# Order of TensorE's steps in the opening: the first up-projection bank of tile 1 ahead of tile 0's rank, the second ahead of tile 1's router

## The chip, the cores and the metric

The kernel runs on one core of a Trainium2 chip. The metric is the time of one execution on the device in microseconds; shown are the median and the spread of several executions. The engines are named as in the profile: PE is TensorE's matmul, PEld its weight load, DVE is VectorE, ACT is ScalarE, POOL is GpSimd, SPq is the queue of SyncE, which issues most transfers.

## The reference

A block of one attention layer and one mixture-of-experts layer, both fed by the same normalised input, over 8 x 512 = 4096 tokens of width 256:

```python
xn = _layernorm(x)
x = x + attn(xn, k, v) + ffn(xn, ...)
# attn: softmax(einsum('bsd,btd->bst', xn, k) * scale) @ v, 1024 keys,
#       scale = xn[:, ::s//4] laid out over the keys
# ffn:  shared = gelu(xf @ Wfc_s + bfc_s) @ Wproj_s + bproj_s       (256 -> 1024 -> 256)
#       probs = softmax(xf @ Wr);  top 2 of 8 experts, weights renormalised
#       routed = sum over e of (gelu(xf @ Wfc[e] + bfc[e]) @ Wproj[e] + bproj[e]) * gate[:, e]
#       return shared + routed
```

## The kernel before

The tokens are cut into 16 tiles of 256. Every float32 product is done as three float16 products: each operand is split into a high and a low half (high x high, high x low, low x high), which the code calls TERMS. The work has stages: for tiles 0 to 7 the shared expert with the routing; attention for 32 blocks of 128 tokens, in whose gaps the other tiles are routed and the expert weights are split and packed; the routed experts over 43 steps of gathered tokens; then the shared expert for tiles 8 to 15. Each engine has its own program written out by hand, and they meet only at semaphores; there is no planner. TensorE's program order is what the change edits.

For each tile of the first stage these steps follow one another over the engines:

- VectorE takes the statistics (front_a with stat), GpSimd the power, VectorE normalises (normalize), ScalarE and VectorE write the high and low half of the rows (split_x_hi, split_x_lo).
- TensorE transposes the tile into PSUM (tr1), and it is copied to x_t: by ScalarE for tiles 0 and 1 (in tile 1's case the copy at L892), by VectorE for the others.
- TensorE does the router's small matmuls (router, L1476). VectorE finds the top two experts and makes a mask (front_a with route, the mask at L1030).
- TensorE does the rank (rank, L1487 to L1490): five matmuls of 8 columns which count, for each token, how many tokens before it go to the same expert. It waits for the mask. VectorE turns this into slot numbers (slots_first at L1053 and L1054, then slots_rest to L1069), and GpSimd scatters the rows (L753).
- TensorE does the up-projection (up_shared, L1513) in four banks of PSUM, each of two hidden chunks and 12 matmuls of 256 columns. ScalarE takes the GELU of each bank and its high half (L858, L864), VectorE the low half (split_h, L1086).
- TensorE does the down-projection. For tile 0 it is cut up in down_first (L1592): the first two terms of each half tile need the high halves of the weights, the third needs their low half, which VectorE makes in split_w1_lo (L1113, two pieces of w_shared[1]; the second one is released to TensorE by s_wlo).

The ps_h bank of a tile may be written again when the GELU of the same bank of the tile before has read it (s_gelu). keep_busy(n) issues n matmuls of 128 columns on the identity, whose result nobody reads.

VectorE's program for the stretch in question, in its order, is:

```python
split_h(0, 0, banks=(0,)); split_x_lo(1)
front_a(route=0); split_w1_lo(0); front_b(route=0)      # front_b: slots_first(0), slots_rest(0)
split_h(0, 0, banks=(1,)); front_a(stat=2); split_h(0, 0, banks=(2, 3))
front_a(route=1); normalize(2); split_h(1, 1, banks=(0,)); split_x_lo(2)
split_w1_lo(1); slots_first(1); copy_xt(2)
```

ScalarE's, from the same point: split_x_hi(1), both scalings of the down weights (L889, L890), the copy of tile 1's x_t (L892), then the GELUs of tile 0's banks 1, 2 and 3, then tile 1's banks 0 and 1, split_x_hi(2) and banks 2 and 3.

Of the kernel before, what the change touches and what calls it, by code (L numbers as in the profile page):

```python
# [68 lines left out]
def moe_attention_block(nc, q, k, v, wfc_s, bfc_s, wproj_s, bproj_s, wr, wfc, bfc, wproj, bproj, out):  # L69
# [30 lines left out]
    with ctx:  # L100
# [1343 lines left out]
        def _(pe):  # L1444
# [14 lines left out]
            def tr1(i):  # L1459
                pe.wait_ge(s_hl, 2 * i)  # L1460
                if i:
                    pe.wait_ge(s_xt, i)
                transpose_quads(x_split[i % 3]).then_inc(s_tr, 1)
# [6 lines left out]
            def router(i, bank=misc):  # L1470
                pe.wait_ge(s_xt, i + 1)
                if 0 < i < NA:
                    pe.wait_ge(s_rb, RB * (i - 1) + 2)
                for a in range(SUB):
                    for n in range(2 * DC):
                        ins = mm(lg_ps(bank)[:, a * 16:(a + 1) * 16], x_t[:, i, n, a * P:(a + 1) * P], wr_s[:, n % DC, :],  # L1476
                                 start=n == 0, stop=n == 2 * DC - 1)
                ins.then_inc(s_logit, 1)

            def rank(i, bank=misc):  # L1480
                par = i % 2
                pe.wait_ge(s_ra, (i + 1) * RA)
                if i:
                    pe.wait_ge(s_rb, (i - 1) * RB + 3)
                for a in range(SUB):
                    o = rk_ps(bank)[:, a * EXPERTS:(a + 1) * EXPERTS]
                    mm(o, before[:, :], mask[par][:, a, :], start=True, stop=False)  # L1487
                    if a == 1:
                        mm(o, ones_h[:, :], mask[par][:, 0, :], start=False, stop=False)
                    ins = mm(o, ones_h[:, :], mask_sum[:, :], start=False, stop=True)  # L1490
                ins.then_inc(s_rank, 1)
# [10 lines left out]
            def up_banks(t, x, w, banks, cols=TILE):  # L1502
                wv = w[:, :].rearrange("p (h c n) -> p h c n", h=2, c=DC)
                for b in banks:
                    if isinstance(t, int) and t == R0:
                        pe.wait_ge(s_mul, QT - 1 + b // 2)
                    elif not (isinstance(t, int) and t == 0):
                        pe.wait_ge(s_gelu, BANKS * (t - 1) + b + 1)
                    for hc in (2 * b, 2 * b + 1):
                        n = 0  # L1510
                        for wl, xl in TERMS:
                            for c in range(DC):
                                ins = mm(ps_h[:, hc * TILE:hc * TILE + cols], wv[:, wl, c, hc * P:(hc + 1) * P],  # L1513
                                         x[:, xl * DC + c, 0:cols], start=n == 0, stop=n == 3 * DC - 1)
                                n += 1
                    ins.then_inc(s_mm1, 1)

            def up_shared(i, t, banks=range(BANKS)):
                pe.wait_ge(s_xt, i + 1)
                up_banks(t, x_t[:, i, :, :], w_shared[0], banks)  # L1520
# [28 lines left out]
            def keep_busy(count):  # L1549

                for n in range(count):
                    mm(ps_v[:, 0:P], ident_h[:, :], ident_h[:, :], start=True, stop=True)
# [23 lines left out]
            router(0)  # L1576
            up_shared(0, 0, (3,))
            tr1(1)
            keep_busy(9)
            rank(0)  # L1580
            keep_busy(6)
            up_shared(1, 1, (0,))
            router(1)

            def down_first(a, terms):
# [7 lines left out]
                                 start=n == 0 and c == 0, stop=n == 2 and c == HC - 1)  # L1593
                return ins

            up_shared(1, 1, (1, 2, 3))
            pe.wait_ge(s_whi, 1)
            down_first(0, (0, 1))
            rank(1)
# [203 lines left out]
```

## Time and profile before

| what | value |
| --- | --- |
| median of 3 runs | 752.18 us (751.36 to 752.41) |
| the profiled execution | 751.78 us |
| its span in the trace | 750.0 us |
| TensorE busy | 738.9 us, 99% of the span |
| VectorE busy | 460.0 us, 61% |
| ScalarE busy | 452.2 us, 60% |
| GpSimd busy | 232.1 us, 31% |

The profiled execution's own time is 1.78 us more than its span. The shares of busy time are averages over all stages; the change lies within the first 30 us. In the rows below, a timeline row has the start and the length in us, the engine, the line, the operation, the tiles written and read, the shapes, and xN for N instructions merged; in brackets is how long the engine had been idle before and what it was released by. The ends of matmuls are modelled, so a row of matmuls overlaps the next one by the time that the last of them takes to drain: the time that a group holds the engine is from its start to the start of the next.

### The profile page before, as it was taken

The page shows a single profiled execution, that of the slowest core. Times are in us where ns is not written, and L with a number is a line of the kernel's source. Part 1 is how long each engine was busy: PE and PEld are TensorE (multiplying, and loading weights), DVE is VectorE, ACT ScalarE, POOL GpSimd, SP SyncE. Part 2 cuts the span into 40 slices and gives each one's busy share as a digit, 9 for nine tenths or more (in the row PEclk, how much of TensorE's full clock was granted, in tenths as well). Part 3 has the DMA queues.
Part 4 walks back from the last instruction along what each step waited for, and adds up shares of the span by engine and source line. Part 5 has one row for each costly group of instructions (what it writes and reads, how often), then busy time and mean ns, then how long its engine had stood idle before and what let it go on. Part 6 is the DMA issues. An engine that isn't in the chain of part 4 may idle for free.

```text
span 750.0 us, 21773 instructions
## 1 busy us (share of the span) xinstructions
PE 738.9 (99%) x7280; PEld 632.5 (84%) x7280; DVE 460.0 (61%) x1200; ACT 452.2 (60%) x903; POOL 232.1 (31%) x275
## 2 busy tenths in 40 slices
PE   6999999999999999999999999999999999999998
PEld 6899977777777777999999999899888888888887
DVE  6888868877777786445454455455444445437766
ACT  6766547666668775466564666665555445554452
POOL 3545426666665663012121211222121221220000
PEclk9999999999999999999999999999999999999999
DMA  9656132748575979554522667533646466205464
GB/s 307 222 187 172 38 141 88 263 160 278 172 248 176 315 257 305 158 170 119 162 49 56 192 190 210 140 103 85 198 136 199 119 177 206 90 27 171 147 211 155
DMA packets 101360, 127.43 MB, mean 170 GB/s; under 512 B 58832, under 2 KB 82992, under 8 KB 94896
## 3 DMA queue, kind: packets, MB, share of 16 engines
q1 hardware_dynamic: 77104, 105.08, 45.7%
q0 software_dynamic: 6368, 17.31, 6.4%
q10 hardware_dynamic: 17824, 4.23, 2.9%
q8 instruction: 35, 0.57, 0.3%
q14 instruction: 29, 0.24, 0.1%
HBM read 85.73 MB, written 40.85 MB: 169 GB/s over the span
## 4 chain that ended last, share of the span: by engine, by line
PE 95%; DVE 2%; ACT 1%; issue 1%; DMA 0%; POOL 0%; DVEq 0%; ACTq 0%; POOLq 0%
PE ps_h L1513 33%; PE ps_v L1533 33%; PE ps_v L1692 11%; PE ps_h L1630 11%; PE ps_t L1644 4%; PE ps_v L1711 1%; PE ps_v L1455 0%; PE ps_t L1455 0%; DMA acc<-in_L_attn_q_dram 0%; ACT h L858 0%; DVE xn L1038 0%; POOL rstd L729 0%; DVE w_shared L1113 0%; PE ps_v L1592 0%; DVE h_split L1086 0%
## 5 line engine op out<-in xcount | busy, mean ns | idle before, releaser
L1086 DVE TENSOR_TENSOR h_split<-h,h_split 128x512 f16<-128x512 f32 (+2 forms) x236 | 140.5, 602 | 138.2 <-ACT h_split L864 136.8
L858 ACT ACTIVATE h<-ps_h,b_fc 128x256 f32<-128x256 f32 (+2 forms) x344 | 127.9, 422 | 141.6 <-PE ps_h L1513 141.5
L1513 PE MATMUL ps_h<-x_t,w_split 128*128 128x256 f16 (+2 forms) x2064 | 185.2, 250 | 1.4 <-DVE x_t L1315 1.2
L1513 PEld LDWEIGHTS ps_h<-x_t,w_split 128*128 128x128 f16 x2064 | 163.8, 98 | 17.5 <-DVE x_t L1315 1.1
L1533 PE MATMUL ps_v<-w_stage,h_split 128*128 128x256 f16 x1536 | 173.6, 273 | 0.0
L799 POOL DMA_INDIRECT tokens_y<-prob,to_i x71 | 73.0, 1028 | 314.1 <-DVE prob L1352 148.9
L1533 PEld LDWEIGHTS ps_v<-w_stage,h_split 128*128 128x128 f16 x1536 | 149.9, 98 | 17.1
L864 ACT CAST h_split<-h 128x512 f16<-128x512 f32 (+2 forms) x236 | 130.1, 551 | 10.6
L1692 PE MATMUL ps_v<-v_split,p_t 128*128 128x256 f16 x768 | 88.9, 272 | 0.0
L1630 PE MATMUL ps_h<-k_t,x_t 128*128 128x512 f16 x384 | 88.1, 379 | 0.0
L858 ACT ACTIVATE h<-ps_h,b_t 128x256 f32<-128x256 f32 x128 | 53.5, 468 | 55.5 <-PE ps_h L1513 55.3
L1513 PE MATMUL ps_h<-x_t,w_shared 128*128 128x256 f16 x756 | 85.4, 273 | 0.0
L1533 PE MATMUL ps_v<-w_shared,h_split 128*128 128x256 f16 x720 | 82.0, 273 | 0.0
L1692 PEld LDWEIGHTS ps_v<-v_split,p_t 128*128 128x128 f16 x768 | 73.6, 98 | 9.8
L1513 PEld LDWEIGHTS ps_h<-x_t,w_shared 128*128 128x128 f16 x756 | 73.3, 98 | 8.4
L1533 PEld LDWEIGHTS ps_v<-w_shared,h_split 128*128 128x128 f16 x720 | 70.2, 98 | 8.5
L753 POOL DMA_INDIRECT slots_x<-x_split,pos_i x64 | 64.7, 1011 | 26.7 <-issue 12.7
L1630 PEld LDWEIGHTS ps_h<-k_t,x_t 128*128 128x128 f16 x384 | 37.6, 98 | 38.1
L912 ACT ACTIVATE prob<-prob,neg_max 128x1024 f32<-128x1024 f32 x32 | 36.8, 1149 | 51.6 <-DVE neg_max L1194 51.6
L1190 DVE CUSTOM_DVE_ANT_0 prob<-ps_h,scale_b 128x1024 f32<-128x1024 f32 x32 | 39.1, 1223 | 23.1 <-PE ps_h L1630 22.9
L1352 DVE SCALAR_TENSOR_TENSOR prob<-ps_v,b_pj 128x256 f32<-128x256 f32 x64 | 26.6, 422 | 36.6 <-PE ps_v L1533 36.1
L1315 DVE STREAM_TRANSPOSE x_t<-x_split 128x1024 f16<-128x1024 f16 (+2 forms) x43 | 43.4, 1009 | 0.0
(184 smaller groups left out, 635.1 us busy)
## 6 DMA issues: line engine op xcount, KB each, us to landing
w_split<-wpack SPq DMA_DIRECT2D x17, 1024.0 KB, 5.6
w_stage<-wpack SPq DMA_DIRECT2D x17, 1024.0 KB, 5.4
wpack<-w_split SPq DMA_DIRECT2D x8, 1024.0 KB, 5.0
wpack<-h_split SPq DMA_DIRECT2D x8, 1024.0 KB, 5.3
y_rows<-tokens_y SPq DMA_DIRECT2D x32, 256.0 KB, 3.2
w_stage<-in_L_ffn_Wfc_dram SPq DMA_DIRECT2D x4, 1024.0 KB, 7.2
scale_b<-key_scale SPq DMA_DIRECT2D x8, 512.0 KB, 8.0
w_stage<-in_L_ffn_Wproj_dram SPq DMA_DIRECT2D x4, 1024.0 KB, 8.4
```

The source lines that it names most:

```text
L753: g.indirect_dma_start(slots_x, bass.IndirectOffsetOnAxis(ap=pos_i[par][:, c:c + 1], axis=0), x_split[i % 3][:, a, :], None).then_inc(s_sc ...
L799: g.indirect_dma_start(tokens_y, bass.IndirectOffsetOnAxis(ap=to_i[par][0:p, a:a + 1], axis=0), y_sb[par][0:p, a, :], None).then_inc(s_y_o ...
L858: ins = nc.scalar.activation(h32[:, hc, 0:n], ps_h[:, hc * TILE:hc * TILE + n], ACT.Gelu_apprx_tanh, bias=bias[:, hc:hc + 1], scale=1.0 / WS)
L864: nc.scalar.copy(h_split[par][:, 0, 2 * b:2 * b + 2, 0:n], h32[:, 2 * b:2 * b + 2, 0:n]).then_inc(s_hhi, 1)
L912: nc.scalar.activation(prob[par][:, :], prob[par][:, :], ACT.Exp, bias=neg_max[par][:, 0:1], accum_out=row_sum[par][:, 0:1]).then_inc(s_ex ...
L1086: ve.tensor_tensor(h_split[par][:, 1, 2 * b:2 * b + 2, 0:n], h32[:, 2 * b:2 * b + 2, 0:n], h_split[par][:, 0, 2 * b:2 * b + 2, 0:n], ALU.s ...
L1190: ve.tensor_tensor_reduce(out=prob[par][:, :], in0=ps_h[:, par * KEYS:(par + 1) * KEYS], in1=scale_b[b % 2][:, :], scale=1.0, scalar=-3.0e ...
L1315: ve.transpose(x_t[:, par, :, 0:n].rearrange("p c (b t) -> p b c t", t=32), x_quad[par][:, 0:n // 32, :].rearrange("p b (r c) -> p b c r", ...
L1513: ins = mm(ps_h[:, hc * TILE:hc * TILE + cols], wv[:, wl, c, hc * P:(hc + 1) * P], x[:, xl * DC + c, 0:cols], start=n == 0, stop=n == 3 * ...
L1533: ins = mm(ps_y[a][:, :], h_split[par][:, xl, c, a * P:(a + 1) * P], wv[:, wl, c, :], start=n == 0, stop=n == 3 * HC - 1)
L1630: ins = mm(ps_h[:, lo:lo + 512], x_t[:, i, ql * DC + c, par * P:(par + 1) * P], k_t[:, kl * DC + c, half * 512:(half + 1) * 512], start=n ...
L1692: ins = mm(ps_y[par][:, :], p_t[par][:, pl, c, :], v_split[:, vl, c, :], start=n == 0, stop=n == 3 * KC - 1)
```

## The change

In TensorE's program for tiles 0 and 1, nine fillers ahead of rank(0) become eighteen, the six behind it go, bank 0 of tile 1 moves from behind rank(0) to ahead of it, and bank 1 of tile 1 from behind router(1) to ahead of it. No instruction of another engine changes.

```diff
             tr1(1)
-            keep_busy(9)
+            keep_busy(18)
+            up_shared(1, 1, (0,))
             rank(0)
-            keep_busy(6)
-            up_shared(1, 1, (0,))
+            up_shared(1, 1, (1,))
             router(1)
...
-            up_shared(1, 1, (1, 2, 3))
+            up_shared(1, 1, (2, 3))
             pe.wait_ge(s_whi, 1)
             down_first(0, (0, 1))
```

## Rows read from the trace of the kernel before

**Rows 1.** The page: its span, and the chain's shares by engine.

```profile
span 750.0 us, 21773 instructions
...
PE 95%; DVE 2%; ACT 1%; issue 1%; DMA 0%; POOL 0%; DVEq 0%; ACTq 0%; POOLq 0%
```

**Rows 2.** What TensorE waited for, whole span: us in total, times, longest.

```profile
PE ps_h L1513 <- DVE x_t L1315: 1.2, 2, 1.0
...
PE ps_t L1487 <- DVE mask L1030: 0.7, 1, 0.7
PE ps_v L1592 <- DVE w_shared L1113: 0.5, 1, 0.5
PE ps_t L1455 <- DVE x_split L1044: 0.3, 1, 0.3
```

**Rows 3.** Timeline of PE, 9 to 29 us.

```profile
9.62 1.48 PE L1565 MATMUL ps_h<-x_t,w_shared 128*128 128x256 f16 x12 [0.99 <-ACT x_t L878]
...
15.71 0.67 PE L1552 MATMUL ps_v<-ident_h 128*128 128x128 f16 x9
17.08 0.18 PE L1487 MATMUL ps_t<-mask,before 128*128 128x8 f16 x1 [0.70 <-DVE mask L1030]
...
17.19 0.17 PE L1490 MATMUL ps_t<-mask_sum,ones_h 128*128 128x8 f16 x1
...
17.55 1.47 PE L1513 MATMUL ps_h<-x_t,w_shared 128*128 128x256 f16 x12
18.86 0.35 PE L1476 MATMUL ps_t<-wr_s,x_t 128*128 128x16 f16 x8
...
22.99 1.91 PE L1592 MATMUL ps_v<-w_shared,h_split 128*128 128x256 f16 x16
...
27.04 0.64 PE L1455 MATMUL ps_t<-ident_h,x_split 128*128 128x128 f16 x8 [0.27 <-DVE x_split L1044]
28.18 1.92 PE L1592 MATMUL ps_v<-w_shared,h_split 128*128 128x256 f16 x16 [0.49 <-DVE w_shared L1113]
```

**Rows 4.** Timeline of all engines, 16 to 28 us: those of DVE and ACT.

```profile
16.19 0.99 ACT L892 COPY x_t<-ps_t 128x1024 f16<-128x1024 f16 x1
...
17.08 0.84 ACT L858 ACTIVATE h<-ps_h,b_t 128x256 f32<-128x256 f32 x2
...
17.95 0.62 ACT L864 CAST h_split<-h 128x512 f16<-128x512 f32 x1
18.07 0.16 DVE L1053 TENSOR_TENSOR mask_sum<-mask_sum,mask 128x8 f16<-128x8 f16 x1
...
19.15 0.69 DVE L1086 TENSOR_TENSOR h_split<-h,h_split 128x512 f16<-128x512 f32 x1
...
21.05 0.18 DVE L1015 BATCH_NORM_AGGREGATE mean_var<-stats 128x2 f32<-128x6 f32 x1 [0.27 <-issue]
...
21.42 1.29 DVE L1086 TENSOR_TENSOR h_split<-h,h_split 128x512 f16<-128x512 f32 x2
...
24.49 0.18 DVE L1030 TENSOR_TENSOR mask<-chosen 128x16 f16<-128x16 f32 x1
...
26.29 0.70 DVE L1044 TENSOR_TENSOR x_split<-xn,x_split 128x512 f16<-128x512 f32 x1 [0.28 <-ACT x_split L840]
26.90 1.22 DVE L1113 SCALAR_TENSOR_TENSOR w_shared<-w_stage,w_shared 128x1024 f16<-128x1024 f32 x1
```

**Rows 5.** The chain that ended last, 16 to 29 us: start, us, what.

```profile
17.02 1.14 DVE w_shared L1113
...
26.99 1.14 DVE w_shared L1113
```

**Rows 6.** Fillers by form, 15.6 to 19.2 and 4 to 8 us: busy us, mean ns.

```profile
L1552 PE MATMUL ps_v<-ident_h 128*128 128x128 f16 x15 | 1.2, 219 | 0.0
...
L1540 PE MATMUL ps_v<-ident_h 128*128 128x128 f16 x31 | 3.5, 313 | 4.2 <-POOL ends L723 4.2
```

**Rows 7.** Windows, 26 to 30 us: busy by engine, granted clock, DMA share, GB/s.

```profile
26.00:30.00 4.00, 3.24 (x35) 2.57 (x33) 3.72 (x9) 2.90 (x7) 2.65 (x2) 1.00 0.44 119
```

## The prediction

> **What bounds the kernel now.** I read the page first, for its span and the chain of work that ended last: TensorE carries 95% of the chain [rows 1]. Then the list of what TensorE waited for. Everything on it but the first wait for constants, at 4.17 us, lies either in the opening or at one point of the routed stage: 1.0 us before tile 0's first up-projection [rows 3], 0.7 us for tile 0's mask, 0.3 us for tile 2's split rows, 0.5 us for the low half of the shared down weights, and 1.2 us for gathered slots far later [rows 2]. Asked for waits from 30 to 400 us, the trace lists none for TensorE. So from 28.18 us on, where the third terms of tile 0's down-projection start, TensorE is dense, and what moves that start moves the end of the kernel by the same amount. The one later wait hangs on engines and transfers that are themselves paced by TensorE's steps, so it moves along and swallows nothing.
>
> Then the opening in order of time. TensorE ends its fillers, waits 0.70 us for the mask, does the five small matmuls of rank(0) at 17.08, six more fillers, bank 0 of tile 1 at 17.55, router(1) at 18.86, the rest of tile 1's banks, and reaches down_first at 22.99; at 27.04 and at 28.18 it stands waiting for VectorE [rows 3]. VectorE in the same stretch goes from one thing to the next [rows 4]. The chain, followed back from 28.18, runs on VectorE: the low half of w_shared[1] at 26.99 is its last piece before TensorE, and from the other half at 17.02 the trace follows it through slots_first(0), the splits of h, the statistics and normalisation of tile 2, with one step over ScalarE (its high half of tile 2's rows) and none over TensorE [rows 5]. So in the opening between 17 and 28 us VectorE sets the pace and TensorE has 0.27 + 0.49 = 0.76 us to spare.
>
> **The change part by part.** (1) Bank 0 of tile 1 moves ahead of rank(0). It needs tile 1's x_t, which ScalarE's copy from 16.19 gives at 16.19 + 0.99 = 17.18 [rows 4]. A step of TensorE that waits for another engine's result starts 0.05 to 0.06 us behind its end (28.12 to 28.18, 26.99 to 27.04 [rows 3, 4]), so bank 0 starts at 17.24 in place of 17.55. Its other condition, the GELU of tile 0's bank 0, is met: ScalarE takes bank 1 at 17.08, and bank 0 stands far ahead of the copy in its program. Gain for TensorE: 0.31 us.
>
> (2) keep_busy(18) in place of 9 and 6. Nine fillers span 0.67 us, of which the last one's own time is 0.22 [rows 3, 6]: 0.45 over eight starts, 0.056 each. Eighteen started at 15.71 take 17 x 0.056 + 0.22 = 1.17 us and end at 16.88, 0.36 us ahead of the copy. They cost nothing; what hides them is that wait. If the fillers went at the slow rate of the first 31 (3.5 us less 0.31, over 30 starts: 0.106 each [rows 6]), the last would start at 17.5 and bank 0 at about 17.6, which would make term 3 worse by 0.37. I don't expect it, since the same fillers in the same place ran at the fast rate. The six fillers behind rank(0) go, 6 x 0.056 = 0.33 us of TensorE time.
>
> (3) rank(0) now stands behind bank 0. A bank's twelve matmuls hold TensorE for 18.86 - 17.55 = 1.31 us [rows 3], so rank(0) starts at 17.24 + 1.31 = 18.55 in place of 17.08, and its last record ends 17.19 + 0.17 - 17.08 = 0.28 us later, at 18.83, in place of 17.36. Who waits for it: slots_first(0) on VectorE, that stands directly behind split_w1_lo(0) in its queue. Before, it started at 18.07 [rows 4], 0.71 us after rank(0) had ended, so the result had that much to spare. Now it can start at 18.83 + 0.05 = 18.88. VectorE stands idle and is 18.88 - 18.07 = **0.81 us late**. Queued behind it are slots_rest(0), the split of h of bank 1 (19.15), tile 2's statistics, the splits of banks 2 and 3, tile 1's routing, and the rest of the chain above.
>
> Is there slack in that queue? The split of bank 1 has its input from ScalarE at 17.95 + 0.62 = 18.57 and yet starts at 19.15, behind the slots [rows 4]; VectorE passes nothing. The Trainium skill, "TensorE: Matmul & The Clock Gate", section "Architectural detail: the array is 16× 32×32, not 1× 128×128", says that VectorE's queue is strictly first in, first out; by that rule the whole 0.81 us is lost, whereas a queue that could pass the waiting step would fill it with the 0.68 us split and lose only 0.13. The trace agrees with the rule at that place. The splits of banks 2 and 3 start at 21.42 with no idle before them; normalize(2) needs GpSimd's power, which is made out of VectorE's own variance, and the 0.28 us before 26.29 is the round trip over ScalarE; both move along. The single gap that need not move is 0.27 us at 21.05, put down to the issue and to no other engine [rows 4]. If it is tied to the clock on the wall (something fetched ahead that the new idle time lets arrive), it is swallowed and the delay is 0.81 - 0.27 = 0.54 us. If it belongs to the instruction it stays. I take it as staying, because the row names no releaser; both ends are kept for the range.
>
> (4) Bank 1 ahead of router(1). Bank 1 starts at 18.55 + 0.14 = 18.69 (its GELU of tile 0's bank 1 must have been read, a step that lasts from 17.08 to 17.92) and router(1) at 20.00 in place of 18.86. Its logits are read by VectorE behind the splits that start at 21.42 and last 1.29, so at about 22.7 before and 23.5 now: covered by more than 3 us, and nothing is late if that cover shrinks by one. Banks 2 and 3 run until 20.00 + 0.2 (router(1)'s 0.35 less the drain of its last) + 2 x 1.31 = 22.82 in place of 22.99.
>
> (5) What TensorE then does. down_first(0) needs all splits of tile 0's h: 21.42 + 1.29 + 0.81 = 23.52, so it starts at 23.57 in place of 22.99 and lasts until 25.3. rank(1) needs the mask that ended at 24.67 [rows 4], now 25.48. The transposes of tile 2 need the split that ended at 26.99, now 27.80, so they start at 27.85; and the third terms need split_w1_lo(1), which ended at 28.12 and now ends at 28.93: start at 28.99 in place of 28.18. TensorE has four short stands in this stretch in place of two, none above 0.7 us, and the 0.31 us and 0.33 us it gained go into them. **Sum:** gain on TensorE 0, VectorE's delay +0.81, end of the kernel +0.81 us, or +0.54 with the gap swallowed.
>
> No transfer is on this way: GpSimd's row ends and scatters of tile 0 start 0.8 us later, but nothing reads the slots before the routed stage. The queue of SyncE has its next loads released by VectorE (the next job's weights behind split_w1_lo(1)) and moves along.
>
> **How the numbers follow.** The profiled execution took 751.78, that is 1.78 us around its span of 750.0. Span 750.0 + 0.81 + 1.78 = 752.59. The median of the runs shown, 752.18, lies 0.40 above the profiled one, and on it the same sum gives 752.99. I predict 753.0. The three runs shown spread over 1.05 us, so from what a measurement can tell, some 0.2% or 1.5 us, this is no change, though on the slow side.
>
> **Rival A, TensorE paces the opening.** If VectorE's lateness were hidden (its queue having slack that the rows don't show, or rank(0) not on its way), the start at 28.18 would follow TensorE's own order, and it would be 0.17 to 0.31 us earlier: 751.9 to 752.0. For it speaks only that TensorE is busy in 95% of the chain; against it that the chain in the opening has no piece of TensorE between 17 and 28 us, and that TensorE stands idle twice in front of VectorE. Chance 0.14, mixtures of the two included.
>
> **Rival B, on the other side: the clock falls.** TensorE now idles more between 22.8 and 29.0: 0.76 us before and about 1.7 us now. If that made its clock fall to the lower of its two levels (1.2 GHz), the dense work behind 29 us would start slow. At the lower level a 128-column filler takes 313 ns and 0.106 us from start to start, at the upper (2.4 GHz) 219 ns and 0.056 us [rows 6]. The slow fillers of the opening last 3.5 us; work for as long as this at the slow rate would lose 3.5 x (1 - 0.056/0.106) = 1.65 us. With the 0.81 this is +2.5, 754.7, slower by 0.3%. It decides when one of the new stands, or their sum, is enough for the clock to fall. Against it: the granted clock is 1.00 from 26 to 30 us in spite of the two stands there [rows 7], and the 0.99 us stand before the first up-projection was followed by twelve matmuls in 1.48 us, as fast as the 1.47 of bank 0 at 17.55 [rows 3]; my longest new stand is 0.7. The Trainium skill, same page, section "HAM oscillation — how this bites in real kernels", warns that stands between short bursts put the clock back to half rate; it speaks of longer ones than I forecast, and by it the change costs nothing here. Chance 0.07.
>
> Other ways to a slower end, a second fetch gap or a transfer that the shift of 0.8 us brings into collision, I give 0.05; and the forecast itself, VectorE late by 0.54 to 0.81 us, has 0.74.
>
> **Chances and range.** Forecast case: 752.7 to 753.0, with a median's own scatter of about 0.5 on either side 752.2 to 753.6. Rival A reaches down to 751.4 with that scatter; rival B lies at 754.7. The range of 8 in 10, 751.6 to 754.2, holds the forecast, most of A, and leaves out B. Over 0.2% faster (under 750.7) no case gives, only scatter: 0.03. Over 0.2% slower (above 753.7): B, the other slower ways and the forecast's upper scatter: 0.07 + 0.02 + 0.04 = 0.13. Within 0.2%: 0.84.
>
> **What would show it.** In the profile of the changed kernel: bank 0 of tile 1 at about 17.24 with a short wait for ScalarE's x_t ahead of it; rank(0) at 18.55 with no wait; a new wait of VectorE's mask_sum for TensorE's rank of about 0.75 us; the wait for the mask gone from TensorE's list and one for h_split of about 0.7 in front of down_first at 23.6; the third terms at 29.0. If the mask_sum step starts at 18.9 but the third terms start before 28.6, VectorE had slack that I didn't see; if they start before 28.2, rival A holds. A 256-column mean well over 272 ns behind 29 us would be rival B. The prediction is wrong altogether if the time past 29 us changes by more than the opening does.

## The result, and the profile after

| | before | after |
| --- | --- | --- |
| median of 20 runs each | 751.77 us (751.3 to 752.73) | 752.59 us (752.06 to 756.64) |
| span of the profiled execution | 750.0 us | 750.9 us |
| TensorE busy | 738.9 us | 739.2 us |

The ratio is 1.0013 with a 95% interval of 1.0007 to 1.0019; the medians differ by 0.82 us. That is slower, but inside the 0.2% that the prediction called no change, and on its slow side. Ratios and intervals, here and below, leave out single slow executions (1999.31 us for one) and are taken over all the others, so they need not be the quotient of two medians. The page of the changed kernel gives the span:

```profile
span 750.9 us, 21780 instructions
```

The list of TensorE's waits over the whole span, without its first row (the constants). The 0.7 us for the mask [rows 2] is gone. In its place stand 0.7 us for the splits of h in front of down_first and 0.4 us for tile 1's x_t; the 0.5 us for the low half of the weights is still there. Far later, in the routed stage, 0.2 us for a transfer of weights is new, while the waits for gathered slots fell from 1.2 to 1.0:

```profile
...
PE ps_h L1513 <- DVE x_t L1315: 1.0, 1, 1.0
PE ps_h L1565 <- ACT x_t L878: 0.9, 1, 0.9
PE ps_v L1592 <- DVE h_split L1086: 0.7, 1, 0.7
PE ps_t L1455 <- DVE x_split L1044: 0.6, 2, 0.3
PE ps_v L1592 <- DVE w_shared L1113: 0.5, 1, 0.5
PE ps_h L1513 <- ACT x_t L892: 0.4, 1, 0.4
PE ps_h L1513 <- DMA w_split<-wpack: 0.2, 1, 0.2
```

The timeline of PE, against [rows 3]:

```profile
15.80 1.17 PE L1552 MATMUL ps_v<-ident_h 128*128 128x128 f16 x18
17.32 1.48 PE L1513 MATMUL ps_h<-x_t,w_shared 128*128 128x256 f16 x12 [0.35 <-ACT x_t L892]
18.64 0.17 PE L1487 MATMUL ps_t<-mask,before 128*128 128x8 f16 x1
...
18.75 0.17 PE L1490 MATMUL ps_t<-mask_sum,ones_h 128*128 128x8 f16 x1
...
20.08 0.35 PE L1476 MATMUL ps_t<-wr_s,x_t 128*128 128x16 f16 x8
20.28 2.78 PE L1513 MATMUL ps_h<-x_t,w_shared 128*128 128x256 f16 x24
23.73 1.91 PE L1592 MATMUL ps_v<-w_shared,h_split 128*128 128x256 f16 x16 [0.67 <-DVE h_split L1086]
...
27.93 0.64 PE L1455 MATMUL ps_t<-ident_h,x_split 128*128 128x128 f16 x8 [0.27 <-DVE x_split L1044]
29.06 1.92 PE L1592 MATMUL ps_v<-w_shared,h_split 128*128 128x256 f16 x16 [0.50 <-DVE w_shared L1113]
30.82 0.35 PE L1476 MATMUL ps_t<-wr_s,x_t 128*128 128x16 f16 x8
```

The timeline of all engines, those of VectorE, against [rows 4]:

```profile
17.02 1.22 DVE L1113 SCALAR_TENSOR_TENSOR w_shared<-w_stage,w_shared 128x1024 f16<-128x1024 f32 x1
...
18.95 0.16 DVE L1053 TENSOR_TENSOR mask_sum<-mask_sum,mask 128x8 f16<-128x8 f16 x1 [0.71 <-PE ps_t L1490]
...
20.04 0.69 DVE L1086 TENSOR_TENSOR h_split<-h,h_split 128x512 f16<-128x512 f32 x1
...
21.93 0.18 DVE L1015 BATCH_NORM_AGGREGATE mean_var<-stats 128x2 f32<-128x6 f32 x1 [0.27 <-issue]
...
22.30 1.28 DVE L1086 TENSOR_TENSOR h_split<-h,h_split 128x512 f16<-128x512 f32 x2
...
27.17 0.70 DVE L1044 TENSOR_TENSOR x_split<-xn,x_split 128x512 f16<-128x512 f32 x1 [0.28 <-ACT x_split L840]
27.78 1.22 DVE L1113 SCALAR_TENSOR_TENSOR w_shared<-w_stage,w_shared 128x1024 f16<-128x1024 f32 x1
```

And two rows of the kernel before, of VectorE's first w_shared piece and of router(2):

```profile
16.94 1.22 DVE L1113 SCALAR_TENSOR_TENSOR w_shared<-w_stage,w_shared 128x1024 f16<-128x1024 f32 x1
```

```profile
29.93 0.35 PE L1476 MATMUL ps_t<-wr_s,x_t 128*128 128x16 f16 x8
```

How to read them: this execution is 0.08 us later than the one before from the start of the stretch (w_shared at 17.02 against 16.94), so each shift below is measured from that row. mask_sum comes 0.80 us later, with a new wait of 0.71 for the last matmul of the rank; the split of bank 1 0.81 later; the second piece of the low half and TensorE's third terms 0.80 later. I call D the distance from VectorE's first w_shared piece to the third terms: 28.18 - 16.94 = 11.24 us before, 29.06 - 17.02 = 12.04 now. And R is the distance from the same row to router(2), from which on TensorE is dense up to the routed stage: 30.82 - 17.02 = 13.80 now, 29.93 - 16.94 = 12.99 before.

One view of the changed kernel misleads. Its chain of work that ended last no longer runs on VectorE throughout; it steps over to ScalarE:

```profile
17.27 0.75 ACT h L858 x2
...
18.66 0.75 ACT h L858 x2
...
20.05 0.67 DVE h_split L1086
```

The split at 20.04 is that of bank 1. The cast that it needs is ScalarE's of bank 1, which ended before 18.7. The trace follows it back to the next cast, bank 2's, only because that one ended at 20.05. By the chain alone one would look for the loss on ScalarE. The experiments below tell where it is.

### The profile page after: what moved, and what is told of

Read it like the earlier page. It is cut to its first block, busy times and chain, and to the rows that moved or that the text cites. A ratio compares the mean times of both kernels' runs of the same rounds, so it can differ in the third digit from the quotient of the medians.

```text
span 750.9 us, 21780 instructions
## 1 busy us (share of the span) xinstructions
PE 739.2 (98%) x7283; PEld 632.1 (84%) x7283; DVE 460.0 (61%) x1200; ACT 451.7 (60%) x903; POOL 233.5 (31%) x275
## 4 chain that ended last, share of the span: by engine, by line
PE 93%; DVE 2%; ACT 2%; DMA 1%; issue 1%; SPq 1%; POOL 0%; DVEq 0%; POOLq 0%; ACTq 0%
PE ps_h L1513 32%; PE ps_v L1533 32%; PE ps_v L1692 11%; PE ps_h L1630 11%; PE ps_t L1644 4%; DMA w_split<-wpack 1%; PE ps_v L1711 1%; ACT h L858 1%; PE ps_v L1455 0%; DMA acc<-in_L_attn_q_dram 0%; PE ps_t L1455 0%; POOL rstd L729 0%; DVE xn L1038 0%; ACT h_split L864 0%; PE ps_v L1592 0%
```

## The experiments

Each was timed beside the kernel before on the same chip, whose median was 751.98 us (30 runs) for the first four, 751.89 (35) for the next four and 751.82 (33) for the last four; the three groups ran on three different chips. D and R come from one profiled execution of each kernel. Line numbers of a changed file can be off by one or two (L1591, L1593 for L1592).

| kernel | median, us (lowest) | ratio, 95% interval | D | R |
| --- | --- | --- | --- | --- |
| bank1_only | 752.16 (751.60) | 1.0002, 0.9993 to 1.0011 | 11.39 | 13.14 |
| bank0_only | 752.55 (752.10) | 1.001, 1.0 to 1.0019 | 12.04 | 13.79 |
| rank_behind_two | 753.69 (753.43) | 1.0029, 1.0019 to 1.004 | 13.35 | |
| stat_first | 751.40 (751.11) | 0.9996, 0.9986 to 1.0005 | 11.14 | 12.90 |
| no_fill | 752.37 (752.07) | 1.001, 0.9999 to 1.0021 | 12.04 | 13.80 |
| tail_before | 750.72 (750.57) | 0.9988, 0.998 to 0.9997 | | 11.94 |
| tail_stat | 750.49 (750.31) | 0.9986, 0.9977 to 0.9995 | | 11.76 |
| fill_gap | 751.35 (751.25) | 0.9994, 0.9985 to 1.0002 | 11.23 | 12.99 |
| change_gap | 752.16 (752.02) | 1.0005, 0.9996 to 1.0015 | 12.03 | 13.78 |
| stat_first_gap | 751.04 (750.81) | 0.9988, 0.9978 to 0.9997 | 10.93 | 12.69 |
| tail_before_gap | 750.57 (750.42) | 0.9983, 0.9974 to 0.9993 | | 11.95 |
| tail_stat_gap | 750.37 (750.24) | 0.9985, 0.9975 to 0.9994 | | 11.77 |

**One part at a time.**

```diff
# bank1_only, against the kernel before
-            up_shared(1, 1, (0,))
+            up_shared(1, 1, (0, 1))
             router(1)
...
-            up_shared(1, 1, (1, 2, 3))
+            up_shared(1, 1, (2, 3))
# bank0_only, against the changed kernel
             rank(0)
-            up_shared(1, 1, (1,))
             router(1)
...
-            up_shared(1, 1, (2, 3))
+            up_shared(1, 1, (1, 2, 3))
```

> One part alone: rank(0) and its fillers stand as before the change, only bank 1 of tile 1 goes ahead of router(1). I measure in the trace the distance D from the start of VectorE's first w_shared[1] low half (17 us) to the start of TensorE's third terms of tile 0's down-projection: 11.24 us before the change, 12.04 after it. Theory (VectorE's wait for rank(0) is the whole loss): no wait of mask_sum for the rank, D 11.2, time within 0.3 us of the kernel before, ratio 1.000. Rival (it is the later router(1), whose logits VectorE reads, that costs): router(1) starts at about 20.2 in place of 18.86 here as well, and D is 12.0, time +0.8 us.

> The other part alone: eighteen fillers, bank 0 of tile 1, rank(0), then router(1) and banks 1, 2, 3. Theory: mask_sum waits 0.7 us for the rank as after the change, D 12.04, time +0.8 us, ratio 1.001. router(1) must now wait for slots_first(0), so TensorE stands about 0.45 us there, but it still reaches down_first before the splits of h are ready, so that costs nothing. Rival (TensorE's own order paces the opening): that stand adds to the loss, D 12.4 to 12.5, time +1.2 us. Rival (the later router(1) is the cost): D 11.3.

bank1_only costs nothing that can be measured (its interval is 0.1% to either side): VectorE's mask_sum (18.80, right behind w_shared at 17.66) has no wait, although router(1) came at 21.29, later than in the changed kernel. D is 11.39, 0.15 above that of the kernel before. That execution had a late start of another kind (last section): ScalarE copied x_t only at 17.59, its cast of bank 1 ended at 19.99, and VectorE's split of that bank, which follows the start of pos_i by 0.08 before, followed it by 0.22. bank0_only has the whole loss. Timelines of its VectorE and TensorE:

```profile
18.86 0.16 DVE L1053 TENSOR_TENSOR mask_sum<-mask_sum,mask 128x8 f16<-128x8 f16 x1 [0.71 <-PE ps_t L1490]
```

```profile
19.25 0.34 PE L1476 MATMUL ps_t<-wr_s,x_t 128*128 128x16 f16 x8 [0.43 <-DVE slot_of L1054]
...
28.97 1.92 PE L1591 MATMUL ps_v<-w_shared,h_split 128*128 128x256 f16 x16 [0.49 <-DVE w_shared L1113]
```

TensorE loses another 0.43 us in front of router(1), and D is 12.04 all the same: an idle TensorE costs nothing here. It also shows what bank 1 ahead of router(1) does in the change: it fills this stand, without a gain.

**The cost enlarged and taken away.**

```diff
# rank_behind_two, against the changed kernel
-            up_shared(1, 1, (0,))
+            up_shared(1, 1, (0, 1))
             rank(0)
-            up_shared(1, 1, (1,))
             router(1)
# stat_first, against the changed kernel, VectorE's program
             split_w1_lo(0)
+            front_a(stat=2)
             front_b(route=0)
             split_h(0, 0, banks=(1,))
-            front_a(stat=2)
```

> The suspected cost is enlarged: banks 0 and 1 of tile 1 both stand ahead of rank(0). Theory: rank(0) comes one more bank, 1.31 us, later, the wait of mask_sum grows from 0.71 to about 2.0 us, D 12.04 + 1.31 = 13.35, time 1.31 us above the changed kernel and +2.1 us above the one before, ratio 1.0028. Rival (the lateness is partly swallowed, the gap of 0.27 us in VectorE's issue first): D 13.1 or less. Rival (TensorE paces the opening, which does the same work in the same time): D stays near 12.0.

> TensorE's order as in the changed kernel, but VectorE does the statistics of tile 2 (about 1.67 us of its time with their pauses, needing nothing of the rank) ahead of slots_first(0) in place of behind the split of bank 1. Theory: they run from 18.1 to 19.8, the rank is ready at 18.9, mask_sum waits for nothing, and D is back at 11.2 to 11.3, time as the kernel before, ratio 1.000. Rival (the loss lies in TensorE's order itself, its clock or a transfer that comes later): D stays at 12.0 and the time at +0.8 us.

rank_behind_two, its timelines of VectorE and TensorE:

```profile
17.14 1.22 DVE L1113 SCALAR_TENSOR_TENSOR w_shared<-w_stage,w_shared 128x1024 f16<-128x1024 f32 x1
...
20.38 0.16 DVE L1053 TENSOR_TENSOR mask_sum<-mask_sum,mask 128x8 f16<-128x8 f16 x1 [2.02 <-PE ps_t L1490]
...
23.36 0.18 DVE L1015 BATCH_NORM_AGGREGATE mean_var<-stats 128x2 f32<-128x6 f32 x1 [0.27 <-issue]
```

```profile
25.16 1.91 PE L1591 MATMUL ps_v<-w_shared,h_split 128*128 128x256 f16 x16 [1.38 <-DVE h_split L1086]
...
30.49 1.70 PE L1591 MATMUL ps_v<-w_shared,h_split 128*128 128x256 f16 x14 [0.49 <-DVE w_shared L1113]
```

The wait grows by 2.02 - 0.71 = 1.31 us, which is one bank, and D by 13.35 - 12.04 = 1.31. Nothing of it is swallowed, and the gap of 0.27 us in front of the second aggregation is still there. The median is 1.71 above the kernel before where 2.1 was expected; the medians carry a scatter of half a microsecond, and lowest against lowest (753.43 against 751.34) it is 2.09.

stat_first keeps TensorE's order and gives VectorE other work during the wait. Its timelines of VectorE and of TensorE:

```profile
17.41 1.22 DVE L1113 SCALAR_TENSOR_TENSOR w_shared<-w_stage,w_shared 128x1024 f16<-128x1024 f32 x1
18.55 0.42 DVE L997 BATCH_NORM_STATS2 stats<-acc 128x6 f32<-128x256 f32 x1
...
19.75 0.17 DVE L1022 TENSOR_SCALAR var_eps<-mean_var 128x2 f32<-128x2 f32 x1
20.03 0.16 DVE L1053 TENSOR_TENSOR mask_sum<-mask_sum,mask 128x8 f16<-128x8 f16 x1
...
21.28 0.17 DVE L1069 CAST pos_i<-pos_all 128x4 int32<-128x4 f32 x1 [0.34 <-DVE pos_all L1067]
```

```profile
19.83 0.17 PE L1490 MATMUL ps_t<-mask_sum,ones_h 128*128 128x8 f16 x1
```

D is 11.14, below the 11.24 of the kernel before. No wait for the rank is listed, but this execution started late (last section): its rank ended only at 19.83 + 0.17 = 20.00, mask_sum follows at 20.03, and it stands 0.28 us behind the start of var_eps. In stat_first_gap (below), the same order without the late start, the rank has ended at 18.81, mask_sum follows var_eps by 0.08, and D is 10.93:

```profile
19.25 0.17 DVE L1022 TENSOR_SCALAR var_eps<-mean_var 128x2 f32<-128x2 f32 x1
19.33 0.16 DVE L1053 TENSOR_TENSOR mask_sum<-mask_sum,mask 128x8 f16<-128x8 f16 x1
```

So 0.2 us of the wait for the rank is left in stat_first, and none in its twin. The loss is gone with this wait though TensorE's order is the changed one: neither ScalarE nor TensorE's order as such holds it.

**The fillers.**

```diff
# no_fill, against the changed kernel
-            keep_busy(18)
```

> The changed kernel without its eighteen fillers, so TensorE stands idle for about 1.1 us ahead of bank 0 of tile 1. Theory (the fillers lie wholly in the wait for x_t and cost nothing): bank 0, rank(0) and the third terms where the changed kernel has them, D (first w_shared[1] low half to the third terms) 12.0 us, time within 0.4 us of the changed kernel, ratio to the kernel before 1.001; the clock stays, 256-column matmuls at 272 ns. Rival (the fillers are what keeps the clock at its upper level there): matmuls of 419 ns behind the stand, which the first up-projection has in some executions, in bank 0 and behind it, and D 13 or more.

Its timeline of TensorE, and its matmuls by form from 17 to 24 us:

```profile
17.12 1.48 PE L1513 MATMUL ps_h<-x_t,w_shared 128*128 128x256 f16 x12 [1.36 <-ACT x_t L892]
```

```profile
L1513 PE MATMUL ps_h<-x_t,w_shared 128*128 128x256 f16 x48 | 5.7, 272 | 1.4 <-ACT x_t L892 1.4
```

With 1.36 us of idle time ahead of bank 0 the clock stayed at its upper level (2.4 GHz), 272 ns for a 256-column matmul. In this execution the eighteen fillers bring nothing, and they cost nothing: the lowest times are 752.07 without and 752.06 with them. It is one profiled execution; that the clock stays in every one isn't shown.

**What VectorE's queue is worth at the other end.**

```diff
# tail_before, against the kernel before; tail_stat has the same edit on stat_first
# VectorE
             normalize(2)
+            split_w1_lo(1)
+            split_x_lo(2)
             split_h(1, 1, banks=(0,))
-            split_x_lo(2)
-            split_w1_lo(1)
# TensorE
-            tr1(2)
             pe.wait_ge(s_wlo, 2)
-            for a in range(SUB):
-                down_first(a, (2,)).then_inc(s_mm2, 1)
+            down_first(0, (2,)).then_inc(s_mm2, 1)
+            tr1(2)
+            down_first(1, (2,)).then_inc(s_mm2, 1)
```

> The kernel before, with only the end of the stretch changed: VectorE does split_w1_lo(1) directly behind normalize(2), in place of the split of h and its wait for ScalarE, and the split of tile 1's bank 0 behind split_x_lo(2); TensorE puts the transposes of tile 2 between the two halves of the third terms. I measure R, from the start of VectorE's first w_shared[1] low half to router(2) on TensorE: 12.99 us before, 13.80 in the changed kernel. Theory (VectorE's queue ahead of the third terms is what TensorE waits for, and from router(2) on TensorE is dense to the end): third terms without a wait, router(2) about 1.0 us earlier, R 12.0, time -1.0 us, 751.0, ratio 0.9987. Rival (the time is given back behind router(2)): R 12.0 but time within 0.3 us of the kernel before.

> The changed kernel's order on TensorE, with tile 2's statistics ahead of slots_first(0) and the end of the stretch as in tail_before. Theory: no wait for the rank on VectorE, and TensorE's earlier bank 0 at last counts, as long as the splits of h are ready at 22.8: R 11.8 to 12.0, time -1.0 to -1.3 us against the kernel before, some 1.9 us below the changed kernel. Rival (the earlier bank 0 is worth nothing whatever VectorE does): R as in tail_before, 12.0.

The timeline of TensorE in tail_before, where the third terms of the first half follow without a wait (24 matmuls in one row), and that of tail_stat:

```profile
24.86 2.78 PE L1592 MATMUL ps_v<-w_shared,h_split 128*128 128x256 f16 x24
27.48 0.61 PE L1455 MATMUL ps_t<-ident_h,x_split 128*128 128x128 f16 x8
27.93 1.04 PE L1592 MATMUL ps_v<-w_shared,h_split 128*128 128x256 f16 x8
28.88 0.36 PE L1476 MATMUL ps_t<-wr_s,x_t 128*128 128x16 f16 x8
...
37.26 0.64 PE L1455 MATMUL ps_t<-ident_h,x_split 128*128 128x128 f16 x8
...
40.36 0.35 PE L1476 MATMUL ps_t<-wr_s,x_t 128*128 128x16 f16 x8
```

```profile
28.75 0.36 PE L1476 MATMUL ps_t<-wr_s,x_t 128*128 128x16 f16 x8
```

router(2) comes 12.99 - 11.94 = 1.05 us earlier. Not all of it is kept: by router(3) 0.84 us is left (40.36 against the row below of the kernel before, each from its w_shared at 16.94). The transposes of tile 3, at 37.26, now start right behind VectorE's split of that tile, which ends at 36.51 + 0.70 = 37.21; before the change this split had ended 0.86 us before they started.

```profile
41.20 0.35 PE L1476 MATMUL ps_t<-wr_s,x_t 128*128 128x16 f16 x8
```

From there to the end of attention nothing more is lost. The medians give 1.17 us, with their scatter; the twins fill_gap and tail_before_gap below, which scatter less, give 751.35 - 750.57 = 0.78. So what is won in VectorE's queue reaches the end but for the 0.2 us for which VectorE is in the way again one tile later. tail_stat adds another 0.18 at router(2).

**The scatter.** In two of the first six profiled executions (the kernel before, the changed one and the first four experiments) the first up-projection had been slow, and this looked like the source of the 1.2 us over which the times of one kernel spread.

```diff
# fill_gap, against the kernel before; the other _gap kernels have the same line
+            keep_busy(9)
             up_first()
```

> The kernel before with nine more fillers ahead of tile 0's first up-projection, in its stand of 0.99 us. In two of six profiled executions the first twelve 256-column matmuls took 419 ns each, in the others 273, and tile 1's transposes then came 1.5 us later and the third terms 0.4 to 0.9 later. Theory (in those executions the clock has not yet risen when the up-projection starts, and more work ahead of it helps it to rise): 273 ns, the lowest time stays near 751.4 and the upper half of the runs (752.0 to 752.6) comes down, median 751.5 or 0.4 us below the kernel before. Rival (when the clock rises does not depend on this stand): the same scatter, same median.

The eleven runs lie between 751.25 and 751.45; those of the kernel before in the same session, one at 755.33 aside, between 751.32 and 752.59. With so little scatter, the change can be priced by times alone:

> The changed kernel with the nine fillers of fill_gap ahead of the first up-projection. Since these took the scatter out of the kernel before (751.25 to 751.45 in 11 runs), the cost of the change can be read from the times themselves: theory 751.35 + 0.81 = 752.16, all runs within 752.0 to 752.4, D (first w_shared[1] low half to the third terms) 12.04 us. Rival (part of the 0.8 is scatter or is given back later): 751.7 or less, or a spread as wide as without the fillers.

> The changed kernel with the nine fillers and tile 2's statistics ahead of slots_first(0). Theory: the wait for the rank is gone, D back at 11.0 to 11.2 us (the 0.27 us issue gap at the second aggregation was not in the trace of stat_first), so 751.35 or up to 0.2 us below it: 751.15 to 751.35. Rival (the change costs something beside the wait for the rank): above 751.6.

change_gap is 752.16 - 751.35 = 0.81 us above fill_gap, the predicted size. That it agrees to the hundredth is luck: the two ran on different chips, and measured from the kernel before on its own chip each, they are 0.34 + 0.54 = 0.88 apart. Nine of change_gap's eleven runs lie between 752.02 and 752.43, the others at 752.80 and, far outside, 2754.95. stat_first_gap is 751.04, 1.12 below change_gap on the same chip, where D differs by 1.10; and its D of 10.93 is 0.30 below that of fill_gap. So its reordering does more than take the wait of 0.8 us away: it also makes VectorE's queue 0.30 us shorter than before the change, which was not expected in this size. The two traces have 0.14 us of it up to tile 1's logits (5.54 us behind w_shared in place of 5.68), 0.12 from there to the mask (1.75 in place of 1.87) and 0.05 from there to the next split of h. The same instructions follow one another faster; why is open.

> The order before the change, the nine fillers, and the end of the stretch as in tail_before. Theory: 751.35 less the 1.04 us that tail_before gained at router(2): 750.3 to 750.6, with the scatter gone. Compared with tail_stat_gap it prices the change's earlier bank 0 once nothing on VectorE is in its way.

> The changed kernel's order with the nine fillers, tile 2's statistics first and the end of the stretch as in tail_before. Theory: TensorE is dense from bank 0 of tile 1 on, which starts at 17.2 with the x_t copy; router(2) comes at 28.6 to 28.75 (28.88 in tail_before, 28.75 in tail_stat), so 0.1 to 0.3 us below tail_before_gap: 750.1 to 750.4, the fastest of all. Rival (the earlier bank 0 is worth nothing whatever VectorE does): equal to tail_before_gap within 0.05.

750.57 and 750.37, 0.20 us apart, with R 11.95 and 11.77, 0.18 apart. So the change's earlier bank 0 has a value, 0.2 us, once VectorE is out of the way: TensorE is dense from bank 0 to router(2) in both, and bank 0 starts 0.31 behind w_shared in place of 0.61, from which rank(0) behind it takes about 0.13 again. And tail_stat_gap is the fastest kernel by its median: 1.8 us below the changed kernel's twin change_gap, and 0.15% (interval 0.06 to 0.25%) below the kernel before. By the intervals it can't be told from tail_before_gap.

## Why the prediction was right, point by point

- The bound: right. TensorE dense from the third terms on, VectorE's queue setting their start. The 0.80 us of D appear as 0.82 in the medians and 0.81 to 0.88 between change_gap and fill_gap. For a gain it holds only in part: of the 1.05 us of tail_before 0.84 is left one tile later.
- Parts 1 and 2: bank 0 at 17.32 - 0.08 = 17.24, as predicted; eighteen fillers in 1.17 us, as worked out. That they cost nothing holds; in no_fill's profiled execution they kept nothing either.
- Part 3, the term that decides: 0.81 predicted, 0.80 in the trace, with a wait of 0.71 where 0.75 stood. VectorE followed the rank's last record by 0.03 us, not 0.05. The choice between 0.81 and 0.54 was right: the gap at the second aggregation stayed at 0.27 us behind the new idle time. rank_behind_two confirms it at 2.02 us of idle.
- Part 4: router(1) at 20.00 on the scale of before, as predicted. bank1_only shows that its cover holds.
- Part 5: third terms at 28.98 on that scale, 28.99 predicted. down_first was put at 23.57, 0.05 behind the last split of h, and came at 23.65, 0.15 behind the split's end (22.30 + 1.28 to 23.73); it isn't shown why, and it costs nothing, since TensorE stands twice more behind it. Of the stands, "none above 0.7" doesn't fit the prediction's own figures, by which the one before down_first is 23.57 - 22.82 = 0.75; it was 0.67.
- That the waits of the routed stage swallow nothing was argued, not worked out. The two executions agree with it: 720.1 us from router(2) to the end in both, with 1.2 us of waits there in both, though 0.2 us of them is now for a transfer where the prediction saw none on the way. Over all kernels this distance is less constant (last section).
- Rival A, TensorE paces the opening: excluded. bank0_only adds 0.43 us of idle TensorE at no cost. Its price for the earlier bank 0 (0.17 to 0.31) is near what the two tail kernels give, 0.2, but only with VectorE's queue shortened.
- Rival B, the clock: did not happen. The stands in the changed kernel are 0.67, 0.27 and 0.50 us in the second half of the stretch, and matmuls of 256 columns take 272 to 273 ns behind them, as in no_fill behind 1.36 us.
- The absolute time, 753.0 against 752.59, was 0.4 too high. The term that was off is the base: the median of the three runs shown, 752.18, lay in the upper part of the scatter, and over 20 runs it is 751.77. 751.77 + 0.81 is 752.58. The profiled execution's sum hits 752.59 exactly, which is luck: that execution, at 751.78, happened to lie at the median of the 20.

## What to carry to other kernels

When a step of one engine is moved behind another, look up when its result is taken, not how long the step lasts: five matmuls of 8 columns, 0.28 us, cost 0.8 us, because a full queue stood behind the wait for them, while the 0.31 us that TensorE gained went into later waits. The chain of waits points at one releaser and can be wrong by a coincidence of ends; moving work that needs nothing ahead of the suspected wait (stat_first) tests it without touching the producer, but look at the whole queue again, since a new order can change more than the wait (0.30 us here). And where the effect is of the size of the scatter, measure distances between two rows of one trace, and look for what makes the scatter.

## What the runs showed of the hardware that was not expected

**A part of the scatter comes from when the clock rises.** The matmuls of the first up-projection by form, 8.5 to 11.9 us, in bank1_only (eleven of the twelve lie in this window) and in fill_gap:

```profile
L1565 PE MATMUL ps_h<-x_t,w_shared 128*128 128x256 f16 x11 | 2.5, 419 | 1.0 <-ACT x_t L878 1.0
```

```profile
L1565 PE MATMUL ps_h<-x_t,w_shared 128*128 128x256 f16 x12 | 1.5, 273 | 0.4 <-ACT x_t L878 0.4
```

419 ns is the lower level (1.2 GHz), 273 the upper. The distance from start to start says the same: (12.15 - 9.62) / 12 = 0.21 us in bank1_only against (10.94 - 9.62) / 12 = 0.11 in the kernel before. In both of these executions, bank1_only's and that of the kernel before, TensorE had done its fillers and eight transposes at the lower level, the eight in 1.06 us, and then stood for x_t for 1.0 us; in the kernel before the clock had risen by the end of this stand, in bank1_only it had not. In bank1_only and stat_first the group took 2.74 us in place of 1.48, tile 1's transposes started at 16.94 and 16.69 in place of 15.24, and VectorE's w_shared at 17.66 and 17.41 in place of 16.94. The granted clock in the row of bank1_only's window, the third number from its end, is 1.00 all the same, so the level has to be read from durations and distances:

```profile
9.00:12.00 3.00, 2.38 (x12) 1.70 (x13) 2.68 (x8) 1.95 (x5) 1.10 (x1) 1.00 1.10 342
```

This happened in 2 of 9 profiled executions without the nine fillers in that stand and in none of 5 with them. The Trainium skill, "TensorE: Matmul & The Clock Gate", section "What's actually happening", says that the moment of the rise varies between runs of one kernel; these traces, of kernels with the same program up to that stand, agree. That the nine fillers make the early rise certain is not shown: 2 of 9 against 0 of 5 can be chance, and in the five executions the fillers themselves already ran at or near the upper level (0.67 to 0.79 us for nine). What speaks for them is the spread, 0.2 us over fill_gap's 11 runs against 1.3, but it is 0.3 to 0.8 in the other four kernels with them (the run at 2754.95 aside).

**Another part arises in the routed stage.** fill_gap's profiled execution took 751.27 us and that of the kernel before 751.78, yet the first up-projection ran at the upper level in both, and router(2) comes at 29.82 and 29.93. The remaining 0.4 us lies behind it: from router(2) to the end of the span it is 749.5 - 29.82 = 719.7 us in fill_gap, 720.1 in the kernel before, 719.6 in bank1_only and 720.3 in stat_first. Up to the scores of the last attention block the executions without the tail edit agree within 0.04 us, counted from router(2). The difference arises later, where the list of TensorE's waits has small entries that are not the same each time (0.2 us for a transfer in the changed kernel, 0.4 us for a split of h in stat_first). So the prediction's "what moves that start moves the end" holds to within some 0.3 us to either side in a single execution, and whether the nine fillers have a part in this too is open.

**The issue gap seems to belong to a place in VectorE's program.** Before the change the 0.27 us put down to the issue stood in front of the eleventh instruction behind w_shared (the second aggregation). In stat_first, whose order differs, the second aggregation has no gap, and 0.34 us stand in front of pos_i, again the eleventh. It neither moved with the clock on the wall nor stuck to the operation. Two orders are few, and what happens at that place no run shows.
